# A fused graph layer on one core: token sums by matmul and a first expert block loaded for every expert

## What is computed

```python
# end of the mixing part, then the layer's sum
h = gelu(h @ fc1_w + fc1_b) @ fc2_w + fc2_b        # 768 -> 3072 -> 768
x = x + gnn(xn) + mix(xn)
y = layernorm(x)                                    # input of the experts
# the expert part, on all 1250 tokens together
pooled = y.mean(axis=tokens)                        # 768 numbers
logits = pooled @ router_w.T + router_b             # 4 experts
top_v, top_i = top_k(logits, 2); gates = softmax(top_v)
out = sum(gates[j] * (act[i](y @ w1[i] + b1[i]) @ w2[i] + b2[i]) for j, i in enumerate(top_i))
x = x + layernorm(out + y)                          # 768 -> 1536 -> 768 per expert
```

## Time and profile before

| | |
|---|---|
| median of 3 runs | 2130.74 us (2129.14 to 2131.43) |
| the profiled execution | 2126.85 us, of which the span of its instructions 2125.1 us |
| PE busy | 1943.3 us, 91% of the span |
| PE weight loads | 1835.3 us, 86% |
| DVE, ACT, POOL busy | 56%, 28%, 26% |
| chain that ended last, by engine | PE 76%, DVE 9%, DMA 5%, ACT 4%, issue 4% |
| mean granted PE clock | 0.96 of full speed |

### The profile page before, as it was taken

One profiled execution on the slowest core, in us unless ns is written; L12 is line 12 of the kernel. 1 busy time (PEld: TensorE's weight loads), 2 busy tenths in 40 slices (PEclk: granted clock), 3 DMA queues, 4 the chain that ended last, 5 costly groups with the idle time before them and its releaser, 6 DMA issues.

```text
span 2125.1 us, 28320 instructions
## 1 busy us (share of the span) xinstructions
PE 1943.3 (91%) x10975; PEld 1835.3 (86%) x10975; DVE 1180.7 (56%) x2061; ACT 594.3 (28%) x1176; POOL 559.8 (26%) x399
## 2 busy tenths in 40 slices
PE   6689979699978899999899999999979999999994
PEld 4367768699968799978899999999979999999994
DVE  7889424688858543377662442442467344274256
ACT  1342202688857431122430110100151001011021
POOL 3332520111100063221331330431206133043045
PEclk9899979799979999999999999999999999999997
DMA  3231220111022331001310210110023011021012
GB/s 123 99 112 69 84 61 1 57 40 59 32 86 94 110 117 45 1 23 60 124 51 23 60 53 8 60 38 23 24 75 102 9 52 60 9 74 45 16 50 111
DMA packets 74476, 124.32 MB, mean 59 GB/s; under 512 B 3297, under 2 KB 45065, under 8 KB 74348
## 3 DMA queue, kind: packets, MB, share of 16 engines
q1 hardware_dynamic: 74348, 122.59, 17.8%
HBM read 97.12 MB, written 25.45 MB: 58 GB/s over the span
## 4 chain that ended last, share of the span: by engine, by line
PE 76%; DVE 9%; DMA 5%; ACT 4%; issue 4%; POOL 1%; DVEq 1%; SPq 0%; ACTq 0%; POOLq 0%
PE pb L965 23%; PE pa L604 22%; PE pb L604 11%; PE pa L657 4%; PE pb L756 3%; PE pb L873 2%; PE pa L743 2%; PE pa L756 2%; DMA md<-md_d 2%; DMA wt_d<-xu 1%; PE pb L774 1%; DVE S1h L1609 1%; DMA xg<-xg_d 1%; ACT sm L1331 1%; DVE st L1871 1%
## 5 line engine op out<-in xcount | busy, mean ns | idle before, releaser
L965 PE MATMUL pb<-X_hi,uw_hi 128*128 128x416 f32 (+1 forms) x864 | 305.4, 353 | 6.1 <-issue 6.1
L965 PE MATMUL pb<-X_hi,uw_lo 128*128 128x416 f32 (+1 forms) x864 | 305.0, 353 | 0.0
L965 PE MATMUL pb<-X_lo,uw_hi 128*128 128x416 f32 (+1 forms) x864 | 304.9, 353 | 0.0
L1524 ACT ACTIVATE tr<-pb,V 128x418 f32<-128x418 f32 (+1 forms) x144 | 87.7, 610 | 768.1 <-PE pb L965 768.0
L604 PE MATMUL pa<-dw_hi,hh 128*125 128x384 f32 x960 | 246.4, 338 | 0.7 <-ACT tr L1524 0.7
L604 PE MATMUL pa<-dw_hi,hl 128*125 128x384 f32 x960 | 245.9, 337 | 0.0
L604 PE MATMUL pa<-dw_lo,hh 128*125 128x384 f32 x960 | 245.9, 337 | 0.0
L1925 DVE CAST hh<-tr 128x418 fp32r<-128x418 f32 (+1 forms) x144 | 115.4, 801 | 220.8 <-ACT tr L1524 220.8
L1083 POOL CAST uw_hi<-raw 128x768 fp32r<-128x768 f32 x48 | 42.9, 895 | 700.7 <-PE pb L965 610.0
L604 PEld LDWEIGHTS pa<-dw_hi,hh 128*125 128x125 f32 x960 | 172.4, 185 | 1.1 <-ACT tr L1524 1.0
L604 PEld LDWEIGHTS pa<-dw_lo,hh 128*125 128x125 f32 x960 | 172.9, 185 | 0.0
(11 more groups left out here) (353 smaller groups left out, 3704.5 us busy)
## 6 DMA issues: line engine op xcount, KB each, us to landing
raw<-in_L_mix_fc_w SPq DMA_DIRECT2D x48, 384.0 KB, 3.3
raw<-in_L_ffn_w SPq DMA_DIRECT2D x48, 384.0 KB, 3.2
md<-md_d SPq DMA_DIRECT2D x20, 610.4 KB
md_d<-mds SPq DMA_DIRECT2D x10, 610.4 KB
raw<-in_L_mix_qkv_w SPq DMA_DIRECT2D x24, 192.0 KB, 5.0
TOK<-in_x SPq DMA_DIRECT2D x10, 375.0 KB
xn_d<-TOK SPq DMA_DIRECT2D x10, 375.0 KB
xu<-in_x SPq DMA_DIRECT2D x10, 375.0 KB
```

Source lines behind the costliest of these rows:

```text
L965: last = nc.tensor.matmul(pb[:, j % 4, 0:n], w_[:, kk, :], x_[:, kk, o:o + n], start=(kk == 0 and q == 0), stop=(kk == KT - 1 and q == 2))
L1524: last = A_(RE[f"tr{j % 3}"][:, 0:w], pb[:, j % 4, 0:w], ACT.Identity if func == "mish" else func, bias=bias(b))
```

## The change

Token sums. `y_features` copies a tile's transposed blocks with two copies (four blocks, two blocks) and no accumulator. The sums come from PE: for each tile, behind its transposes, six matmuls with the tile of TK as weights (125x128) and a column of ones moving, into six columns of PSUM beside the transposes; ScalarE copies these six numbers to `psums`. The last tile's sums run ahead of its transposes, into another bank, and VectorE adds them to the mean of the other nine directly.

First block. SP loads block 0 of all four experts (4 x 384 KB) into a new buffer `pre` as soon as the last first-layer job of group 5 and its parts are done. When `r_idx` is there, ScalarE reads the first expert's number and makes the high part of its block by a copy, VectorE the low part by a subtraction. `raw` no longer carries this block; POOL starts with block 1, once the first block has been counted and all tiles are split.

Order. On ScalarE the features of tile 8 come ahead of the root of tile 9, and the block's copy ahead of the exponential. On VectorE the scales of tile 9 come ahead of the split of tile 7; the splits of tiles 8 and 9 come behind the block's low part, and the gates behind those splits. PE waits for tile parts chunk by chunk in group 6 (four tiles, then seven, then all), and its wait for the gates stays where it was.

```diff
@@ sp
+            sp.wait_ge(*at("up_mm", JOBS * MLP_GROUPS))
+            sp.wait_ge(*at("h_lo", JOBS * MLP_GROUPS))
+            for e in range(EXP):
+                sp.dma_start(RE["pre"][:, e, :].rearrange("p (k n) -> p k n", k=KT), w1e[:, e, :, 0:P]).then_inc(sem("pre_in"), 16)
             for t in range(NT):
                 sp.wait_ge(*at("dn_acc", NT * (MLP_GROUPS - 1) + t + 1))
@@
-                    for b in range(GK):
+                    for b in range(0 if e or g else 1, GK):
@@ pe
             def norm_transposes(t):
                 pe.wait_ge(*at("y_xh", t + 1))
+                if t == NT - 1:
+                    pe.wait_ge(*at("dn_acc", NT * MLP_GROUPS - 1))
+                    column_sums(pa[:, 0, :], t).then_inc(sem("y_sum"), 1)
                 if t >= 2:
                     pe.wait_ge(*at("y_ev", t - 1))
-                back_to_features(TK[:, t, :], t).then_inc(sem("y_tr"), 1)
+                last = back_to_features(TK[:, t, :], t)
+                if t < NT - 1:
+                    last = column_sums(pb[:, 2 * (t % 2) + 1, 2 * TP:], t)
+                last.then_inc(sem("y_tr"), 1)
+
+            def column_sums(bank, t):
+
+                for m in range(KT):
+                    last = nc.tensor.matmul(bank[:, m:m + 1], TK[:, t, m * P:(m + 1) * P], ones[0:TP, 0:1], start=True, stop=True)
+                return last
@@
             pe.wait_ge(*at("r_gates", 1))
             nc.tensor.matmul(pa[:, 0, 8:8 + TOPK], ones_row[:], rt[0:1, 20:20 + TOPK], start=True, stop=True).then_inc(sem("r_gb"), 1)
-            pe.wait_ge(*at("y_x", NT))
+            def first_expert_group(n):
+
+                if n < 2:
+                    pe.wait_ge(*at("y_x", (7, NT)[n]))
+
+            pe.wait_ge(*at("y_ev", NT - 1))
+            pe.wait_ge(*at("y_x", 4))
@@ pool
                     pool.wait_ge(*at("y_x", NT))
-                for b in range(GK):
+                    pool.wait_ge(*at("bw_split", up_page(g, 0) + 1))
+                for b in range(1 if g == MLP_GROUPS else 0, GK):
                     up_split(g, b)
@@ act
-                for m in range(KT):
-                    last = A_(RE[f"ftx{t % 2}"][:, m, :], six(pb[:, 2 * (t % 2), :], pb[:, 2 * (t % 2) + 1, :], m), ACT.Copy,
-                              accum_out=psums[:, t, m:m + 1])
+                bank4, bank2 = pb[:, 2 * (t % 2), :], pb[:, 2 * (t % 2) + 1, :]
+                A_(RE[f"ftx{t % 2}"][:, 0:4, :], bank4[:, 0:4 * TP].rearrange("p (m n) -> p m n", m=4), ACT.Copy)
+                last = A_(RE[f"ftx{t % 2}"][:, 4:6, :], bank2[:, 0:2 * TP].rearrange("p (m n) -> p m n", m=2), ACT.Copy)
+                if t < NT - 1:
+                    last = A_(psums[:, t, :], bank2[:, 2 * TP:2 * TP + KT], ACT.Copy)
@@
             y_features(NT - 1)
+            for q in range(2):
+                act.wait_ge(*at(f"x2_out{q}", 16 * len(range(q, NT, 3))))
+            act.wait_ge(*at("pre_in", 16 * EXP))
+            act.wait_ge(*at("r_idx", 1))
+            first = act.value_load(rti[0:1, 0:1], min_val=0, max_val=EXP - 1)
+            A_(uw[0][0][:], RE["pre"][:, ds(first, 1), :].rearrange("p e (k n) -> p (e k) n", k=KT), ACT.Copy).then_inc(sem("pre_hi"), 1)
             act.wait_ge(*at("r_d", 1))
             A_(rt[0:1, 17:18], rt[0:1, 16:17], ACT.Exp).then_inc(sem("r_e"), 1)
@@ dve
-            dve.wait_ge(*at("y_ev", NT))
-            ch.link(v.tensor_reduce(pooled[:], psums[:].rearrange("p i k -> p k i"), AX.X, ALU.add))
-            v.tensor_scalar(pooled[:], pooled[:], 1.0 / N, None, ALU.mult).then_inc(sem("r_pool"), 1)
-            split_tile(NT - 1, RE["ftx1"][:], "y_ev", "y_x")
+            dve.wait_ge(*at("y_ev", NT - 1))
+            ch.link(v.tensor_reduce(pooled[:], psums[:, 0:NT - 1, :].rearrange("p i k -> p k i"), AX.X, ALU.add))
+            ch.link(v.tensor_scalar(pooled[:], pooled[:], 1.0 / N, None, ALU.mult))
+            dve.wait_ge(*at("y_sum", 1))
+            v.scalar_tensor_tensor(out=pooled[:], in0=pa[:, 0, 0:KT], scalar=1.0 / N, in1=pooled[:], op0=ALU.mult, op1=ALU.add
+                                   ).then_inc(sem("r_pool"), 1)
@@
             v.tensor_tensor(rt[0:1, 16:17], rt[0:1, 9:10], rt[0:1, 8:9], ALU.subtract).then_inc(sem("r_d"), 1)
+            dve.wait_ge(*at("r_idx", 1))
+            first = dve.value_load(rti[0:1, 0:1], min_val=0, max_val=EXP - 1)
+            dve.wait_ge(*at("pre_hi", 1))
+            v.scalar_tensor_tensor(out=uw[0][1][:], in0=RE["pre"][:, ds(first, 1), :].rearrange("p e (k n) -> p (e k) n", k=KT), scalar=1.0,
+                                   in1=uw[0][0][:].bitcast(fp32), op0=ALU.mult, op1=ALU.subtract).then_inc(sem("bw_split"), 1)
+            split_tile(NT - 2, RE["ftx0"][:], "y_ev", "y_x")
+            split_tile(NT - 1, RE["ftx1"][:], "y_ev", "y_x")
             dve.wait_ge(*at("r_e", 1))
```

More of the change, by code:

```diff
@@ L88, in page_loads @@
 def page_loads(i):
-    return 2 if PG_KV <= i < PG_Q else 1
+    return 2 if PG_KV <= i < PG_Q else 0 if i == up_page(MLP_GROUPS, 0) else 1
 def page_landed(i):
@@ L308, in gps_layer @@
                   + [(f"tr{q}", [P, CH], fp32) for q in range(3)] + [("m_e", [P, CH], fp32), ("m_n", [P, CH], fp32)],
-                  [(f"x2s{q}", [TP, D], fp32) for q in range(3)] + [(f"ftx{q}", [P, KT, TP], fp32) for q in range(2)])
+                  [(f"x2s{q}", [TP, D], fp32) for q in range(3)] + [(f"ftx{q}", [P, KT, TP], fp32) for q in range(2)]
+                  + [("pre", [P, EXP, D], fp32)])
         X_hi, X_lo, TOK, G, TK = RX["X_hi"], RX["X_lo"], RT["TOK"], RT["G"], RT["TK"]
@@ L555, in _ @@
                     page_load(down_page(g, k), (raw[down_page(g, k) % NRAW][:], fc2[GK * g + k]))
+            w1e = A["ffn_w1"].rearrange("e (k p) n -> p e k n", p=P)
+            w2e = A["ffn_w2"].rearrange("e (k p) n -> p e k n", p=P)
+            sp.wait_ge(*at("up_mm", JOBS * MLP_GROUPS))
+            sp.wait_ge(*at("h_lo", JOBS * MLP_GROUPS))
+            for e in range(EXP):
+                sp.dma_start(RE["pre"][:, e, :].rearrange("p (k n) -> p k n", k=KT), w1e[:, e, :, 0:P]).then_inc(sem("pre_in"), 16)
             for t in range(NT):
@@ L560, in _ @@
             sp.wait_ge(*at("r_idx", 1))
-            w1e = A["ffn_w1"].rearrange("e (k p) n -> p e k n", p=P)
-            w2e = A["ffn_w2"].rearrange("e (k p) n -> p e k n", p=P)
             for e in range(TOPK):
@@ L1026, in _ @@
             nc.tensor.matmul(pa[:, 0, 8:8 + TOPK], ones_row[:], rt[0:1, 20:20 + TOPK], start=True, stop=True).then_inc(sem("r_gb"), 1)
-            pe.wait_ge(*at("y_x", NT))
+            def first_expert_group(n):
[3 more added lines that the diff above has]
+            pe.wait_ge(*at("y_x", 4))
             for g in range(MLP_GROUPS, ALL_GROUPS):
-                group_jobs(g)
+                if g == MLP_GROUPS:
+                    group_jobs(g, first_expert_group)
+                else:
+                    group_jobs(g)
                 for t in range(NT):
@@ L1533, in _ @@
             for t in range(NT):
+                if t == NT - 1:
+                    y_features(t - 1)
                 root("y", t, "eps5")
-                if t >= 1:
+                if 1 <= t < NT - 1:
                     y_features(t - 1)
@@ L1538, in _ @@
             y_features(NT - 1)
+            for q in range(2):
[4 more added lines that the diff above has]
+            A_(uw[0][0][:], RE["pre"][:, ds(first, 1), :].rearrange("p e (k n) -> p (e k) n", k=KT), ACT.Copy).then_inc(sem("pre_hi"), 1)
             act.wait_ge(*at("r_d", 1))
             A_(rt[0:1, 17:18], rt[0:1, 16:17], ACT.Exp).then_inc(sem("r_e"), 1)
-            act.wait_ge(*at("r_idx", 1))
             for e in range(TOPK):
@@ L1956, in _ @@
                 moments("y", t, x2s[t % 3][:])
+                if t == NT - 1:
+                    scales("y", t)
                 if t >= 2:
                     split_tile(t - 2, RE[f"ftx{t % 2}"][:], "y_ev", "y_x")
-                scales("y", t)
-            split_tile(NT - 2, RE["ftx0"][:], "y_ev", "y_x")
-            dve.wait_ge(*at("y_ev", NT))
-            ch.link(v.tensor_reduce(pooled[:], psums[:].rearrange("p i k -> p k i"), AX.X, ALU.add))
-            v.tensor_scalar(pooled[:], pooled[:], 1.0 / N, None, ALU.mult).then_inc(sem("r_pool"), 1)
-            split_tile(NT - 1, RE["ftx1"][:], "y_ev", "y_x")
+                if t < NT - 1:
+                    scales("y", t)
+            dve.wait_ge(*at("y_ev", NT - 1))
[4 more added lines that the diff above has]
+                                   ).then_inc(sem("r_pool"), 1)
             dve.wait_ge(*at("r_log", 1))
```

## The result

| | before | changed |
|---|---|---|
| median of 8 runs each | 2129.39 us | 2135.19 us |
| lowest to highest | 2128.60 to 2131.43 | 2133.01 to 2139.83 |
| profiled execution, span | 2126.85, 2125.1 | 2139.83, 2138.1 |
| PE busy | 1943.3 us | 1967.3 us |

The ratio is 1.0026, 95% interval 1.0017 to 1.0035: slower by 5.8 us where 5.5 were forecast.

What follows compares the result with a forecast made beforehand. PE, busy 91% of the span, was taken to bound the kernel. Loop +8.1 and tail -2.6 made +5.5 us, put on a median of 2130.74: 2136.2 us (+0.26%), range 2130 to 2141.

Steps and rivals of the forecast that it cites:

- The bound of the loop: Group 5's ten second-layer jobs: 5.14 us a tile, 4.84 PE's own work, 0.3 waiting for TK from ScalarE.
- The price of a tile's sums: Six sums on PE: twelve weight loads at 0.108, 1.30 us a tile, between bounds of 0.3 and 2.3.
- Period and loop: Second-layer loop: tile period 6.13 us instead of 5.14, making the loop 8.1 us longer.
- The tail: From T to the experts' first matmul: T+15.15 instead of T+17.74, 2.6 us sooner.
- T: End of the tenth second-layer job of the first MLP's last group; tail times count from it.
- rival 3: Tail: PE clock already at 0.50 at the last sums, total +7.3 us, 2138.0; chance 0.12.
- What is late next: At the experts' start: the gates, not the first block, hold PE; block at T+10.95, experts at T+15.15.
- Loads and queues: Early block loads, x2 writes and POOL's next block: none on the path; first x2 write some 3 us later at worst.
- Clock at the experts' start: Experts' first group starts at clock 0.50 again; its 2.6 us loss is kept, ±0.9.
- The sum: Whole kernel: +8.1 - 2.6 = +5.5 us; chance 0.67 of slower, with the 0.2% bound at 2135.0 us.

Runs made afterwards that it cites:

- scales_first: pool_acc with every tile's two normalization scalars ahead of VectorE's split of the tile two before; loop 47.7 us, ratio to before 0.9963.
- pool_acc: gates_late with POOL adding up the tiles and TensorE summing that total once, tile 9 separately; loop 49.3 us, ratio to before 0.9974.
- one_sum: Changed kernel with only one of the six sums for tiles 0 to 8; loop 50.4 us, ratio to before 0.9994.
- merged: Changed kernel with transposes and sums in one pass of 126 moving columns, twelve weight loads a tile; loop 53.2 us, ratio to before 1.0004.
- sums_only: Kernel before with the token sums on TensorE and their order, first expert block loaded and split as before; ratio to before 1.0034.
- gates_late: Changed kernel with PE's wait for the gates and the gates' matmul moved behind the experts' first job; ratio to before 1.0015.
- pool_acc_warm: pool_acc with spare matmuls in two of PE's waits of the tail, nine and seventeen; ratio to before 0.9971.
- router_first: scales_first with tile 9's transposes behind the router's matmuls and its features behind the first block's copy; ratio to before 0.9953.
- block_only: Changed kernel with sums back on ScalarE's accumulators and the mean over ten tiles on VectorE; loop 49.8 us, ratio to before 0.9995.

## Why the prediction was right, point by point

**The bound of the loop.** Right in what mattered: 4.84 us of PE work in 5.14, so new PE work of 1.3 us is paid but for 0.3. The 4.84 was seen bare in scales_first. Incomplete was whom PE waited for. The prediction named ScalarE; pool_acc showed two chains of nearly equal length, ScalarE's copies and VectorE's split.

**The price of a tile's sums.** 1.30 was taken between bounds of 0.3 and 2.3; 1.34 was measured, twelve steps of 0.112 (1.24 of it on the sums' own line of the chain). The choice of the nearest rows, by the width of the weights and not by the number of moving columns, was the step that decided the sign, and one_sum and merged bear it out. The evidence for it was thinner than the text says: 97 columns are a quarter fewer than 130, not a third, and their step was 0.108 against 0.112.

**Period and loop.** 6.13 forecast, 6.19 measured (1584.70 to 1590.89); +8.1 forecast, +8.6 measured. What was too small is the price of one load: 12 x 0.112 makes 1.34 where 1.30 was taken. The other terms held, 0.64 for the transposes and 4.21 for the job, where 4.27 less 0.08 was taken.

**The tail.** -2.6 forecast, -2.5 measured, and that close only by luck, with errors that cancel. ScalarE and VectorE were faster (TK of tile 9 at T+4.5 instead of 4.9; the block 2.9 us behind r_idx as forecast, with 0.84 for its copy instead of 1.0), and PE slower: the clock fell during the last sums, so that they took 1.63 instead of 1.47 and the transposes 1.49 instead of the 0.8 to 0.9 of the earlier trace rows. r_idx came at T+8.5 instead of 8.0, and the splits and gates behind it gave 0.4 back. This is rival 3 in part. Tile 8's sums, at the full clock, lasted 1.40; the last sums took 2.07 us in sums_only and 2.2 to 2.7 in the profiles of gates_late, one_sum, pool_acc, pool_acc_warm, scales_first and router_first, where one in eight had been given to such a fall. It was the worst-judged chance: gates_late runs the same instructions up to there, and in its execution the tail's gain of 2.5 would have been 1.4.

**What is late next.** The gates, as said: 3.85 us behind the block here, and gates_late took their place away.

**Loads and queues.** Nothing of them cost: block_only's loop is the loop of before. POOL's next block never showed in a chain, in router_first neither, where its cover was least.

**Clock at the experts' start.** The first group took 43.2 us, 0.5 less than in the earlier trace rows: where the loss of 2.6 us was kept, 2.1 was lost. That is within the ±0.9.

**The sum.** +5.5 forecast, +5.8 in the medians. The chance of 0.67 was given to slower by over 0.2%; the ratio lies above that bound and the interval reaches below it.

What stays open: why executions of one kernel differ by 4 to 9 us ahead of this stretch. The profiles place most of it in the stages before 1075 us (the first MLP's first matmul starts at 1068.85 before and at 1074.65 in the changed kernel), and no run here was made for it.

## What to carry to other kernels

Where an engine is busy 94% of a loop, work moved onto it is paid but for what the loop had to spare (1.05 us of 1.34 a tile here), whatever it relieves; ask first which engine is idle there (POOL's adding of the tiles never stood in pool_acc's chain, and TensorE then had one total to sum). The small matmuls here were priced by their weights, up to about as many moving columns as weight columns: load the wide operand once and let everything it must meet, an identity and a column of ones, move past it in one pass. When a late transfer is taken off a path, look at what the same engine was told to do in the meantime: the gates had been 6 us early and became the new wait by an order of five instructions.

## What the runs showed of the hardware that I had not expected

A plain fp32 matmul with 125x128 weights takes two instructions, and each takes 0.112 us whether one column moves (the changed kernel) or 126 (merged). The limit is above that: in another stage of the kernel before, twenty instructions with 193 moving columns take 562.18 to 565.45, 0.163 each.

```profile
562.18 3.43 PE L756 MATMUL pa<-G,PT 125*125 125x193 f32 x20
565.45 1.25 PE L743 MATMUL pa<-ident,sm 125*125 125x125 f32 x10
```

PE can be busy without its clock staying up. In pool_acc_warm it was busy 5.00 of 5 us from 1585 to 1590, with the last of nine spare matmuls, twelve one-column sums, six transposes and the router's twelve, and stood at 0.50 all the time; it rose only during the seventeen spare matmuls behind them, of 384 columns each. It had fallen at 1584 to 1585, with the first of the nine spare matmuls already running, behind a wait of 1.1 us and twelve one-column sums. In pool_acc, without spare matmuls, the granted clock from 1583 to 1585 was 1.00. Which of these instructions let the clock fall is not shown.
